# A DLRM tower on one core: layer 2's weights turned inside the loop, and its last step in high and low parts

## The reference

```
Xi = X0 = e                                   # [512, 39, 16]
for W, b in ((W0,b0),(W1,b1),(W2,b2)):        # W: [128, 39*Fi]
    Xi = einsum('hjk,bjd,bkd->bhd', W.reshape(128, 39, Fi), X0, Xi) + b
    res.append(Xi.sum(axis=2))                # [512, 128]
h = concat(res + [dense_ctx], axis=1)         # [512, 400]
h = relu(h @ W_top1 + b_top1); h = relu(h @ W_top2 + b_top2); y = h @ W_top3
```

## Time and profile before

| | |
|---|---|
| median of 3 runs | 709.32 us (709.06 to 712.4) |
| the profiled execution's own time | 708.21 us |
| its span, first to last instruction | 706.4 us |
| busy share of PE, ACT, DVE, POOL | 95%, 77%, 67%, 64% |
| first product of the loop, last product of the loop | 48.2 us, 649.2 us |

### The profile page before, as it was taken

How to read it: one execution, slowest core, us unless ns; L and a number is a source line. 1 busy time by engine, 2 the same in 40 slices (tenths; PEclk the granted TensorE clock), 3 DMA queues, 4 the chain that set the end, 5 groups by cost and what they waited for, 6 DMA issues and landing times. The chain is left out here.

```text
span 706.4 us, 10134 instructions
## 1 busy us (share of the span) xinstructions
PE 673.8 (95%) x2647; PEld 484.4 (69%) x2647; DVE 476.2 (67%) x928; ACT 546.4 (77%) x1958; POOL 454.9 (64%) x445
## 2 busy tenths in 40 slices
PE   4478899999999999999999999999999999999998
PEld 4266667777777777777777777777777777776443
DVE  3256777777787778778777777777877777887000
ACT  3346788888898888988888889888988898998003
POOL 6516847777878787877887878777877555322000
PEclk9669899999999999999999999999999999999999
DMA  8244131312131312212121313131313140300000
GB/s 294 59 165 145 9 95 5 95 6 94 6 95 7 94 8 70 31 47 54 30 71 15 85 7 94 6 94 8 95 6 95 5 158 10 143 5 0 1 0 0
DMA packets 99163, 40.77 MB, mean 58 GB/s; under 512 B 80593, under 2 KB 84957, under 8 KB 98850
## 3 DMA queue, kind: packets, MB, share of 16 engines
q1 hardware_dynamic: 93059, 37.58, 20.2%
q0 software_dynamic: 5120, 1.29, 2.1%
q10 hardware_dynamic: 927, 1.26, 0.6%
HBM read 11.26 MB, written 2.56 MB: 20 GB/s over the span
## 5 line engine op out<-in xcount | busy, mean ns | idle before, releaser
L508 ACT ACTIVATE prod<-ps_y,xt 128x128 f32<-128x128 f32 x1792 | 493.9, 435 | 79.0 <-PE ps_y L831 64.5
L829 PE MATMUL ps_y<-w_hi,x_hi 128*128 128x512 f32 (+1 forms) x640 | 312.0, 488 | 6.4 <-ACT prod L508 3.6
L830 PE MATMUL ps_y<-w_lo,x_hi 128*128 128x512 f32 (+1 forms) x640 | 249.7, 390 | 0.0
L831 PE MATMUL ps_y<-w_hi,x_lo 128*128 128x512 f32 (+1 forms) x640 | 249.3, 390 | 0.0
L369 POOL TENSOR_TENSOR prod<-prod 128x512 f32<-128x512 f32 x120 | 155.1, 1292 | 114.0 <-ACT prod L508 107.1
L679 DVE SCALAR_TENSOR_TENSOR prod<-ps_y,xt,prod 128x128 f32<-128x128 f32 x576 | 164.6, 344 | 55.2 <-PE ps_y L831 47.8
L340 POOL DMA_INDIRECT rows<-in_table,index x160 | 155.5, 972 | 39.1 <-issue 32.9
L829 PEld LDWEIGHTS ps_y<-w_hi,x_hi 128*128 128x128 f32 x640 | 120.8, 189 | 67.0 <-issue 23.9
L686 DVE TENSOR_REDUCE prod<-prod 128x128 f32<-128x1536 f32 (+1 forms) x64 | 116.3, 1818 | 60.1 <-ACT prod L508 60.1
L830 PEld LDWEIGHTS ps_y<-w_lo,x_hi 128*128 128x128 f32 x640 | 121.1, 189 | 47.5 <-issue 23.9
L364 POOL TENSOR_TENSOR room<-room 117x512 f32<-117x512 f32 (+1 forms) x105 | 135.3, 1292 | 14.7 <-DMA room<-room 14.7
(11 more groups left out here) (99 smaller groups left out, 245.6 us busy)
## 6 DMA issues: line engine op xcount, KB each, us to landing
room<-room SPq DMA_DIRECT2D x75, 234.0 KB
room<-room SPq DMA_DIRECT2D x45, 78.0 KB
emb_room<-rows SPq DMA_DIRECT2D x168, 5.0 KB
rows<-in_table,index POOLq DMA_INDIRECT x160
w2t_dram<-g_all SPq DMA_DIRECT2D x1, 2496.0 KB, 9.1
room<-w2t_dram SPq DMA_DIRECT2D x1, 2496.0 KB, 9.2
room<-room SPq DMA_DIRECT2D x15, 156.0 KB
g_all<-in_L_rec_W SPq DMA_DIRECT2D x9, 256.0 KB
```

The lines of the kernel that those rows point to most:

```text
L508: ins = nc.scalar.activation(prod[:, SLOT[k] + m // 2, :, m % 2], ps_y[:, g % YBANKS, m * H:(m + 1) * H], ACT.Copy, scale=xt[:, q % 2, ti, ...
L829: nc.tensor.matmul(y, hi, w1_hi[:, cols], start=True, stop=False)
L830: nc.tensor.matmul(y, hi, w1_lo[:, cols], start=False, stop=False)
L831: nc.tensor.matmul(y, lo, w1_hi[:, cols], start=False, stop=True).then_inc(y_made, 1)
```

## The change

W2 leaves the preparation: no load, turn, copy or write of it stands ahead of the loop, and W1's loads take the place of its loads on SP. The remaining thirteen groups use seven banks instead of five.

W2 is instead loaded in five parts in quads 1 to 5, into the half of `g_all` that the second half of the batch fills later; turned four fields at a time into `ps_tr` in the last tile of a quad and the first of the next (ten turns, tiles 7 to 24, behind the fifth group); split there by ACT into a high part and by DVE into a low part; and written to DRAM, both parts, by SP in quads 4 to 8. In the last tile both parts are read back, over `w1_hi` and `w1_lo`, part by part as layer 1 is through with the columns.

The last step makes three float32r products for each field. ACT makes the high part of that field's plane, DVE the low part, in a ring of four. All eight known MLP products stand behind the loop, four ahead of the last `sum_d` and four behind it.

```diff
-TURNS = ([("w2", g) for g in range(GROUPS)] + [("w1", g) for g in range(4)] + [("w0", 0), ("w0", 1)]
-         + [("w1", g) for g in range(4, GROUPS)] + [("dense", 0)])
+TURNS = ([("w1", g) for g in range(4)] + [("w0", 0), ("w0", 1)] + [("w1", g) for g in range(4, GROUPS)]
+         + [("dense", 0)])
+PREP_BANKS = YBANKS + 2
+W2_SIZE = 4
+W2_TURNED_IN = {QT * (n // 2 + 1 + n % 2) + (0 if n % 2 else 3): n for n in range(W2_GROUPS)}
+W2_TURNED_AFTER = 4
+W2_SAVED_BEHIND = 4
+HALF = B // 2
+RING = 4
...
+        w2_hi, w2_lo = w1_hi, w1_lo
+        g_hi = sb("g_hi", [P, RING, B], F32R)
+        g_lo = [x[:, par, :] for par in range(2) for x in (x1_hi, x1_lo)]
...
+                if q <= W2_PARTS:
+                    if q == 1:
+                        sp.wait_ge(prep_tr, len(TURNS))
+                    load_w2(q - 1)
+                if 0 <= q - W2_SAVED_BEHIND < W2_PARTS:
+                    save_w2(q - W2_SAVED_BEHIND)
...
-            sp.wait_ge(w2_saved, 16)
-            sp.wait_ge(z_used, CHUNKS * QUADS)
-            sp.wait_ge(xt_turned, QUADS)
-            sp.dma_start(w2t, w2t_dram).then_inc(late_w2, 16)
+            sp.wait_ge(w2_saved, 32 * W2_PARTS)
+            for n in range(GROUPS // 2):
+                sp.wait_ge(y_made, GROUPS * (TILES - 1) + 2 * n + 2)
+                cols = slice(FIRST[2 * n] * H, (FIRST[2 * n + 1] + SIZES[2 * n + 1]) * H)
+                for low, dst in enumerate((w2_hi, w2_lo)):
+                    sp.dma_start(dst[:, cols].bitcast(F32), w2_dram[low][:, cols]).then_inc(late_w2[n], 16)
...
+                    if g == 6 and T in W2_TURNED_IN:
+                        n = W2_TURNED_IN[T]
+                        act.wait_ge(w2_turned, n + 1)
+                        nc.scalar.copy(w2_home(False, n).bitcast(F32R),
+                                       ps_tr[:].rearrange("p (r c) -> p r c", c=HALF)).then_inc(w2_hi_made, 1)
             keep_g(TILES - 1)
+            act.wait_ge(g_kept, TILES)
+            for j in range(F):
+                wait(act, g_used, j - RING + 1)
+                nc.scalar.copy(g_hi[:, j % RING, :], g_all[:, j, :]).then_inc(g_hi_made, 1)
...
+                if T in W2_TURNED_IN:
+                    n = W2_TURNED_IN[T]
+                    dve.wait_ge(w2_hi_made, n + 1)
+                    nc.vector.tensor_tensor(w2_home(True, n).bitcast(F32R),
+                                            ps_tr[:].rearrange("p (r c) -> p r c", c=HALF),
+                                            w2_home(False, n), ALU.subtract).then_inc(w2_lo_made, 1)
             reduce_late(TILES - 1)
+            for j in range(F):
+                dve.wait_ge(g_hi_made, j + 1)
+                nc.vector.tensor_tensor(g_lo[j % RING], g_all[:, j, :], g_hi[:, j % RING, :].bitcast(F32),
+                                        ALU.subtract).then_inc(g_lo_made, 1)
...
             def turn_x(q):
                 pe.wait_ge(x0_made, q + 1)
+                wait(pe, w2_lo_made, sum(T <= QT * (q - 1) for T in W2_TURNED_IN))
+            def turn_w2(T):
+                n = W2_TURNED_IN[T]
+                wait(pe, w2_lo_made, n)
+                src = w2_home(True, n)
+                for m in range(min(W2_SIZE, F - W2_SIZE * n)):
+                    ins = nc.tensor.transpose(ps_tr[:, m * H:(m + 1) * H],
+                                              src[:, m // 2, m % 2 * H:(m % 2 + 1) * H], ident[:])
+                ins.then_inc(w2_turned, 1)
...
             for j in range(F):
-                ins = nc.tensor.matmul(ps_r3, w2t[:, j * H:(j + 1) * H], g_all[:, j, :], start=j == 0, stop=j == F - 1)
+                pe.wait_ge(late_w2[part], 32)
+                pe.wait_ge(g_lo_made, j + 1)
+                nc.tensor.matmul(ps_r3, w_hi, g_hi[:, j % RING, :], start=j == 0, stop=False)
+                nc.tensor.matmul(ps_r3, w_lo, g_hi[:, j % RING, :], start=False, stop=False)
+                nc.tensor.matmul(ps_r3, w_hi, g_lo[j % RING], start=False, stop=j == F - 1).then_inc(g_used, 1)
```

More of the change, by code:

```diff
@@ L119, in build @@
     MC1, MC2 = M1 // P, M2 // P
-    w2t_dram = nc.dram_tensor("w2t_dram", (P, F * H), F32, kind="Internal").ap()
+    w2_dram = [nc.dram_tensor(f"w2_{what}_dram", (P, W2_GROUPS * W2_SIZE * H), F32, kind="Internal").ap()
+               for what in ("hi", "lo")]
     with ExitStack() as ctx:
@@ L282, in _ @@
             sp.dma_start(b1_row[:], b1.rearrange("(a h) -> a h", a=1).broadcast_to([P, H])).then_inc(small_ld, 16)
-            for n in range(W2_PARTS):
-                cols = slice(FIRST[2 * n] * H, (FIRST[2 * n + 1] + SIZES[2 * n + 1]) * H)
-                sp.dma_start(w2_in[:, cols], W2[:, cols]).then_inc(w2_ld[n], 16)
             for g in range(GROUPS):
@@ L863, in _ @@
                         turn_x(q + 1)
+                    if T in W2_TURNED_IN and g == W2_TURNED_AFTER:
+                        turn_w2(T)
                     if g == SUM_D_AFTER and T > 0:
```

111 lines of the change are left out of this document (64 added, 47 removed).

## The result

| | before | after |
|---|---|---|
| median of the runs (us) | 709.38 (709.06 to 712.40) | 702.08 (701.21 to 703.25) |
| the profiled execution: own time, span | 708.21, 706.4 | 701.35, 699.5 |
| PE busy in the span | 673.8 | 666.5 |

The ratio is 0.9877, 95% interval 0.9846 to 0.9907. The change makes the kernel 1.2% faster, 7 us of the 17.5 that the forecast gave it, and the time lies 0.08 above the upper end of the range.

What follows compares the result with a forecast made beforehand. PE was taken to bound the loop, a W1 handover round the start, and float32 products the end. Own time 708.21 - 17.9 + 7.3 - 6.9 = 690.7, as median 691.8 us; range 685 to 702.

Steps and rivals of the forecast that it cites:

- minus 17.9: Start: preparation ends at 18.0, before quad 0's rows at 18.9, so everything from 36.78 to the loop moves 17.9 us earlier.
- ACT's 1.55: Start: ACT's idle time ahead of each W1 group before the change, once with releaser "remote"; if kept, minus 8.3 only.
- Rival 4: Start: first tile waits for POOL's second set of gathers, no gain; chance 0.04 together with a mixture near no change.
- The turns, plus 7.3: Loop: ten groups of W2 turns in PE's full stretch cost 0.73 each, plus 7.3 us, bounds 5.0 and 7.9.
- The 0.79: Loop: upper bound for one group of W2 turns, from four turns of the embeddings, 1.02 - 0.23.
- The 23 turns in 3.07: Loop: W2's own turns at the start, 0.126 each or 0.50 for four, taken as the lower bound.
- The cover of the turns: Loop: ACT's ten copies, DVE's ten subtractions and SP's loads and saves fit beside PE and cost nothing.
- The end, minus 6.9: End: from 43.2 to 36.3 us, with eight known products 8.4, `sum_d` 0.54 and 117 field products 27.4.
- Rival 1: Start stays paced: preparation keeps 2.14 us per W1 group, minus 8.3 instead of 17.9, 701.4 us; chance 0.26.
- Rival 2: Last step: late PE signals slow the ring of four; at 2.14 per field the kernel takes 748 us; chance 0.04.
- rival 3: Quad 0: PE's 3.58 wait for ACT in tile 1 or 2 vanishes too, 684.8 us; chance 0.08.

Runs made afterwards that it cites:

- e1: Changed kernel with quad 1's gathers held on POOL until the first tile's chain is through; 694.68 us, ratio 0.9816 to the kernel before.
- e14: e1 unaltered, run again on chip X; 692.33 us, ratio 1.0039 to the kernel before on that chip.
- e2: Kernel before the change with quad 1's gathers held until the preparation's end; 704.16 us, ratio 0.9944.
- e5: Changed kernel run again unaltered; 700.85 us, ratio 0.9867 to the kernel before.
- e16: Changed kernel unaltered, run once more beside the kernel before; 700.85 us, ratio 0.9887.
- e18: Changed kernel unaltered, run once more; 701.29 us, ratio 0.9884 to the kernel before.
- e6: Changed kernel with quad 1's gathers held only until quad 0's rows are turned; 696.57 us, ratio 0.9803 to the kernel before.
- e10: e1 with five of quad 2's ten gathers alternating with POOL's multiplications; 705.65 us, ratio 0.9951 to the kernel before.
- e8: Changed kernel with four of the eight known MLP products back in the last quad's tiles; 701.30 us, ratio 0.9847 to the kernel before.
- e13: Changed kernel, seven of quad 1's gathers held behind the first tile's chain, quad 2's in two rows of five, on chip X; 688.56 us, ratio 0.9982.
- e17: e13's kernel once more, not on chip X; 694.60 us, ratio 0.9786 to the kernel before.

## Why the prediction was wrong, point by point

- **"The start is then bound by the gathers. Everything from 36.78 to the loop hangs on those rows and moves with them: minus 17.9."** This is the step that failed: -9.4 on the chips measured. The arithmetic of the bound holds where PE's signals are on time: -18.2 in e1, by two errors of 1.2 and 1.4 that cancel (rows later, chain shorter), and in e14 the preparation ends at 17.8. What was left out is that the chain behind the rows now runs beside quad 1's gathers, where before it ran, from 36.8 on, behind them. It went from 11.4 to 16.6, and the rows were taken up at 22.1, not 18.9. e2 shows the same from the other side: there the rows are taken up 10.5 earlier with W2's loads and turns still in place, and the chain behind them takes 16.2. The row for it was in hand, ACT's 1.55 "for which I have no cause", and I took the value that needed no lateness.
- **Nothing was put down for tiles 0 to 4.** They gave back 5.0 (2.4 to 6.6 in the six other traces of the same program up to there). 1.3 of it is lost in tile 0. The wait in tile 1 costs nothing against the kernel before, which has it too: the lead is 8.1 at tile 1 and 9.2 at tile 2. The rest, 4.7, goes in tiles 3 and 4 and is new: late signals in tiles 2 and 3 (up to 5.2 behind PE, beside quad 3's gathers), which then make SP's and POOL's work for quad 2 late: PE waits 1.53 at 85.96, 0.87 at 94.99 and 1.73 at 99.09. And the assumption behind the sum, that a gain at the first product stays, is weak by itself: e1 has 18.2 there and 9.3 at tile 1, because quad 1's rows are a second chain. Rival 4 named that chain and then set it at nothing.
- **The turns, plus 7.3.** They cost 4.2, 0.42 a group against 0.73 and against a lower bound of 0.50: this term of the sum was mis-sized by 3.1. The 0.79 came from turns that read with gaps; with a contiguous source four take 0.354, 0.088 each on average. The 23 turns in 3.07 were no lower bound: at 0.126 each they were evidently not PE's own pace. The Trainium skill's 275 ns for a turn ("TensorE: Matmul & The Clock Gate", Part 4: PE-mode transpose) is the length of one, not its cost: by the groups of PE each of the 39 turns is 270 to 273 ns long, yet the next one starts 108 to 110 ns behind it, and the product behind the last of four 28 to 30 ns behind that (the row at 135.69 has four in 0.35).
- **The cover of the turns held.** ACT is busy 478.89 of 540, DVE 417.75, PE 539.84: copies, subtractions and SP's transfers cost nothing, `turn_x` never waits.
- **The end, minus 6.9.** Right: 6.4 to 6.9 from tile 28 to the end in e5, e16 and e18. Its two parts were off in opposite directions, and that they cancel is luck: the known products out of the last quad give 3.1 to 3.7 where 4.2 was put down, and from the last group's start on it is 54.3 in those three against 57.6 before, 3.3 where 2.7 was put down. In the first trace the clock was at its half level from 652.6 to 656.0, and the first fields' products stand 0.43 apart instead of 0.23, so that one shows 5.2 in all. Fields are 0.687 apart, DVE and ACT keep up, and no field waits for the read-back.
- **The rivals.** Rival 1 came near in its time (701.4) and its cause is the one that decided, but at another place: W1's groups went through at under 0.9 us each until 16.7, and of the 8.5 that are missing 3.2 lie in the rows' take-up and 5.2 in the chain behind it. Against it I had argued that nine groups went through quickly "with the same gathers running"; they were the first 6 us of the row that starts at 11.6. Its chance of 0.26 was too low for something that stood in the trace twice. That 701.4 lies so near the measured 702.08 is luck: the start gave 9.4 and not 8.3, tiles 0 to 4, for which rival 1 had nothing, took 5.0, and tiles 5 to 28, turns included, cost 2.7 where it had 7.3. Rival 2's ring did not come late, rival 3's pause is still there (3.54), and rival 4's gathers were not slowed.

## What to carry to other kernels

An idle time that a profile puts down to "remote", or to an engine that had long ended, is a cost of its own: look for what runs beside each of its places, and before moving a chain ask whether it moves beside that. When a start is brought forward, follow the second tile's or quad's inputs as well as the first's. And take a gain at the start as local to the chip until a second chip has shown it: what a fixed wait buys on one can cost time on another.

## What the runs showed of the hardware

- In a row of gathers issued by POOL each 1.25 us, PE's semaphore signals reach ACT and DVE up to 7.4 us behind the product's start (e6, tile 1), beginning 4 to 10 us into the row and ending 1 to 3 us behind it, and then in a burst (five in 0.3 us). PE itself runs on. The length of the row is not all there is to it: the rows of ten beside tile 0 of e1 (30.4 to 43.1) and of e10 (33.1 to 45.4) show none as far as PE works beside them, 9 us into each, and the kernel before has signals 2.3 to 2.5 late in tile 11 in its three traces, beside a row of only four. The path that is blocked is not shown by any run, and all times here are of executions with the profiler's records, of which a fifth to over a quarter is missing on these chips; that the recording has a part in it is not excluded.
- It was there in each of the eighteen traces from elsewhere and in neither of the two from chip X, where the kernel before takes 689.7 instead of 707.7 to 710.8. That difference of 19 us is as large as the whole of what the change was made for; that it is all lateness is argued, not shown, since no trace of the kernel before exists from chip X. The nearest measure is e2, whose preparation alone is 10.5 shorter with the row out of its way.
- The granted clock stood at the half level for 3.4 us at the beginning of the last step in four of the sixteen traces with this step (after, e8, e13, e17), with the same work before it in others that kept the full clock. By the stretch from the last group's start to the end, 56.0 against 54.3, it costs 1.6.
